# Four half buffers of edge features and four groups of accumulators in a graph kernel on one Trainium2 core

## The reference, cut to what matters

```
msg  = leaky_relu([x[dst], edge_attr] @ w1 + b1) @ w2 + b2    # layer 0
agg0 = segment_sum(msg, src)
coef = rel_table[edge_type]                                    # layer 1: weight of an edge
out1 = segment_sum(coef * alpha * z[src], dst)
out2 = segment_sum(h[src] * norm, dst)                         # layer 2
out3 = segment_sum(h[src], dst) / degree                       # layer 3
```

## Time and profile before

| | us |
|---|---|
| median of three runs | 4012.09 (4009.74 to 4016.07) |
| profiled execution, its own time | 4007.71 |
| its span, first to last instruction | 4006.0 |
| first and last indirect DMA of the scatter | 278.0 and 1541.3 |
| first and last sum of the edge tiles on DVE | 1560.5 and 3032.7 |

### The profile page before, as it was taken

How to read it: one execution, slowest core, us unless ns; L and a number is a source line. 1 busy time by engine, 2 the same in 40 slices (tenths; PEclk the granted TensorE clock), 3 DMA queues, 4 the chain that set the end, 5 groups by cost and what they waited for, 6 DMA issues and landing times. The chain is left out here.

```text
span 4006.0 us, 89562 instructions
## 1 busy us (share of the span) xinstructions
PE 2767.3 (69%) x19674; PEld 2009.0 (50%) x19675; DVE 2620.8 (65%) x7923; ACT 1608.0 (40%) x4084; POOL 1983.2 (50%) x2354
## 2 busy tenths in 40 slices
PE   2314554455454555888888888888888967769599
PEld 2213333333333334787777877787785222234345
DVE  8724555555555554888888888888886759950501
ACT  1001222222222223776777777776775613320201
POOL 0015666566666666777777777777772000000100
PEclk9955556666666657999999999999999979979797
DMA  9971222221222223777777777777774848848082
GB/s 387 415 291 59 65 65 63 64 62 61 64 64 65 65 64 106 205 203 202 204 204 203 202 206 202 202 205 197 202 206 171 294 173 295 296 151 325 22 325 100
DMA packets 702415, 696.60 MB, mean 174 GB/s; under 512 B 51182, under 2 KB 633536, under 8 KB 692640
## 3 DMA queue, kind: packets, MB, share of 16 engines
q1 hardware_dynamic: 672706, 637.13, 50.5%
q0 software_dynamic: 25792, 54.52, 4.0%
q10 hardware_dynamic: 3870, 4.37, 0.3%
HBM read 340.91 MB, written 354.90 MB: 174 GB/s over the span
## 5 line engine op out<-in xcount | busy, mean ns | idle before, releaser
L885 POOL DMA_INDIRECT sorted_rows<-rows,posi x806 | 779.8, 967 | 577.1 <-issue 246.4
L836 PE MATMUL s_peq<-sb_w1bb,eT 128*128 128x256 f32 x806 | 395.5, 591 | 584.9 <-ACT eT L703 359.6
L1166 DVE SCALAR_TENSOR_TENSOR acc<-acc,keep,pm 128x256 f32<-128x256 f32 x1504 | 717.4, 477 | 76.3 <-DVE acc L1166 36.3
L997 POOL TENSOR_SCALAR ohs_e<-iota,rt 128x128 f32<-128x128 f32 x1128 | 669.6, 608 | 11.4 <-DMA rt<-sorted_rows 11.4
L1093 PE MATMUL pm<-ohw_e,ohs_e 128*128 128x128 f32 x3008 | 662.7, 302 | 0.0
L1006 POOL TENSOR_TENSOR hid<-pre_e,excess 128x512 f32<-128x512 f32 x376 | 498.7, 1326 | 313.5 <-ACT excess L1033 313.5
L836 PEld LDWEIGHTS s_peq<-sb_w1bb,eT 128*128 128x128 f32 x806 | 188.9, 288 | 635.3 <-ACT eT L703 398.7
L1099 PE MATMUL px<-PN,dT 128*128 x4512 | 498.5, 219 | 0.2 <-ACT dT L1040 0.2
L1049 ACT ACTIVATE ohw_e<-ohd_e,rt 128x128 f32<-128x128 bf16 x1504 | 474.6, 386 | 0.0
L1092 PE MATMUL pm<-ohd_e,ohs_e 128*128 128x128 bf16 x1504 | 334.3, 222 | 198.1 <-DVE acc L1166 182.8
L1093 PEld LDWEIGHTS pm<-ohw_e,ohs_e 128*128 128x128 f32 x3008 | 459.7, 193 | 0.0
(11 more groups left out here) (299 smaller groups left out, 4469.3 us busy)
## 6 DMA issues: line engine op xcount, KB each, us to landing
count_matrices<-acc SPq DMA_DIRECT2D x1504, 128.0 KB, 2.0
ab<-count_matrices SPq DMA_DIRECT2D x75, 1600.0 KB, 7.8
sorted_rows<-zrow SPq DMA_DIRECT2D x188, 528.0 KB, 9.9
rt<-sorted_rows SPq DMA_DIRECT2D x376, 264.0 KB, 3.0
arb<-count_matrices SPq DMA_DIRECT2D x25, 1664.0 KB, 6.8
arb<-count_matrices SPq DMA_DIRECT2D x25, 1536.0 KB, 6.4
ef<-in_edge_attr_dram SPq DMA_DIRECT2D x60, 364.0 KB
sorted_rows<-rows,posi POOLq DMA_INDIRECT x806
```

The source lines that it names most:

```text
L836: nc.tensor.matmul(pe_q[:, q % 2, 0:2 * D], eT[:, q % 2, :], w1bb[:], start=True, stop=True).then_inc(s_q, 1)
L885: pool.indirect_dma_start(sortd, bass.IndirectOffsetOnAxis(ap=posi[:, h, c:c + 1], axis=0), rows[:, h, c, :], None).then_inc(s_sc[h], 16)
L997: last = nc.gpsimd.tensor_scalar(ohs[:, k, j, :], iota128[:], rt[:, k, j, D + 1:D + 2], None, ALU.is_equal)
L1166: nc.vector.scalar_tensor_tensor(acc[:, k % 2, j, :], before, keep[:, at:at + 1] if isinstance(at, int) else keep[:, ds(at, 1)], pm[:, j / ...
```

## The change: deeper rings in two parts, and another order on DVE

Scatter: `ef` gets four halves (two bodies of two). SP may load a half for body i when PE has turned the same half of body i-2; ACT loads the first two bodies, not one, at the start. The loops of SP and PE now run over two bodies a pass.

Edge tiles: `rt` gets eight groups, and the loops run over eight groups a pass on all engines. The one-hot buffers stay at four (BUFS). `acc` gets four groups (SUMS), with one semaphore a group in place of one a tile: `collect` 0 waits until all four writes of group n-4 have landed, the other three wait for none. Dummy places go from 8 to 16. On DVE collect 2 moves ahead of the destination one-hots, and collect 3 ahead of the sums.

```diff
-RING = 4
+RING = 8
+BUFS = 4
+SUMS = 4
...
-                ef = sb2("ef", [P, 2, CH, ED])
+                ef = sb2("ef", [P, 2, 2, CH, ED])
...
-                    with sp.Fori(1, whole) as i:
+                    even = whole // 2 * 2
+                    with sp.Fori(1, even // 2) as m:
+                        for b in range(2):
+                            for h in range(2):
+                                sp.wait_ge(s_te, (m * 2 + b - 2) * PAIRS + (MEET + 1, PAIRS)[h])
+                                load(sp, m * 2 + b, b, h)
+                                load_last(sp, m * 2 + b, b, h, CH)
...
-                    for h in range(2):
-                        load(act, 0, h)
-                        load_last(act, 0, h, CH)
+                    for b in range(2):
+                        for h in range(2):
+                            load(act, b, b, h)
+                            load_last(act, b, b, h, CH)
...
-                    with pe.Fori(1, BODIES - 1) as i:
-                        step(i, False, False)
+                    with pe.Fori(1, BODIES // 2) as m:
+                        for b in range(2):
+                            step(m * 2 + b, m, b, False, False)
...
-            ohd = sb("ohd_e", [P, RING, G, P], BF16)
+            ohd = sb("ohd_e", [P, BUFS, G, P], BF16)
...
-            acc = sb("acc", [P, 2, G, 2 * P])
+            acc = sb("acc", [P, SUMS, G, 2 * P])
...
-            s_w = [[sem("e_written%d_%d" % (p, j)) for j in range(G)] for p in range(2)]
+            s_w = [sem("e_written%d" % p) for p in range(SUMS)]
...
-                                     acc[:, k % 2, j, :].rearrange("p (a c) -> p a c", a=2)).then_inc(s_w[k % 2][j], 16)
+                                     acc[:, k % SUMS, j, :].rearrange("p (a c) -> p a c", a=2)).then_inc(s_w[k % SUMS], 16)
...
-                    if not (first and k < 2):
-                        dve.wait_ge(s_w[k % 2][j], (i * 2 + k // 2) * 16)
+                    if j == 0 and not (first and k < SUMS):
+                        dve.wait_ge(s_w[k % SUMS], (i * (RING // SUMS) + k // SUMS) * (16 * G))
...
                     if three:
                         st = place(*back(i, k, 3))
+                    if two:
+                        collect(*back(i, k, 2), first, 2)
                     if not (final and k >= RING - 2):
                         onehots(*back(i, k, -2), first and k + 2 < RING)
                     if two:
-                        collect(*back(i, k, 2), first, 2)
+                        collect(*back(i, k, 2), first, 3)
                     if three:
                         sums(*back(i, k, 3), first, st)
-                    if two:
-                        collect(*back(i, k, 2), first, 3)
```

More of the change, by code:

```diff
@@ L602, in build @@
                 lk = pb2("s_looked", [P, BANK])
-                s_row = [sem("s_row_a"), sem("s_row_b")]
+                s_row = [[sem("s_row%d_%d" % (b, h)) for h in range(2)] for b in range(2)]
                 s_tl = sem("s_tables_in")
@@ L625, in build @@
                 block = ctx.enter_context(nc.Block())
-                efv = ef[:].rearrange("p h c d -> p (h c d)")
+                efv = [ef[:, b, :, :, :].rearrange("p h c d -> p (h c d)") for b in range(2)]
                 rowv = rows[:].rearrange("p h c w -> p (h c) w")
@@ L956, in step @@
                     n = i * RING + k
-                    rows = loads(nc, mybir.EngineType.SP, tilei[0:1, 2, ds(n * G, G)], DUMMY + 2 * G - 1)
+                    rows = loads(nc, mybir.EngineType.SP, tilei[0:1, 2, ds(n * G, G)], DUMMY + SUMS * G - 1)
                     for j in range(G):
@@ L982, in _ @@
                     step(LOOPS - 1, k, False)
-                for p in range(2):
-                    for j in range(G):
-                        sp.wait_ge(s_w[p][j], 16 * LOOPS * RING // 2)
+                for p in range(SUMS):
+                    sp.wait_ge(s_w[p], 16 * G * (LOOPS * RING // SUMS))
             @block.gpsimd
@@ L1042, in step @@
                         negative(*back(i, k, 1), first)
-                    if not first:
-                        act.wait_ge(s_m, 2 * (n - RING) + 2)
+                    if not (first and k < BUFS):
+                        act.wait_ge(s_m, 2 * (n - BUFS) + 2)
                     act.wait_ge(s_os, n + 1)
                     act.wait_ge(s_o3, n + 1)
-                    nc.scalar.activation(ohs16[:, k, :, :], ohs[:, k, :, :], ACT.Copy).then_inc(s_o16, 1)
+                    nc.scalar.activation(ohs16[:, k % BUFS, :, :], ohs[:, k % BUFS, :, :], ACT.Copy).then_inc(s_o16, 1)
                     for j in range(G):
-                        last = nc.scalar.activation(ohw[:, k, j, :], ohd[:, k, j, :], ACT.Copy, scale=rt[:, k, j, D + 2:D + 3])
+                        last = nc.scalar.activation(ohw[:, k % BUFS, j, :], ohd[:, k % BUFS, j, :], ACT.Copy, scale=rt[:, k, j, D + 2:D + 3])
                     last.then_inc(s_ow, 1)
```

76 lines of the change are left out of this document (37 added, 39 removed).

## The result

The changed kernel takes 3949.61 us (median of four runs, 3944.23 to 3951.51); the kernel before took 4010.91 beside it (4009.32 to 4016.07). The ratio is 0.9843, with a 95% interval of 0.9825 to 0.9861. The forecast was 3969, with a range of 3938 to 4006. The profiled execution took 3951.51 us with a span of 3949.8, against 4007.71 and 4006.0 before: 56.2 us less, where the sum said 43.

What follows compares the result with a forecast made beforehand. The prediction took SP's issuing queue to bound the edge tiles and POOL to pace the scatter. Terms -54 + 7 + 1.8 + 2.0 = -43 us took 4012 to 3969 us, range 3938 to 4006.

Steps and rivals of the forecast that it cites:

- SP's queue bounds the edge tiles: Edge tiles: SP's issuing needs at least 3.83 us a group of 3.92; DVE's wait for `rt` is an effect.
- The floor, -54: Edge tiles: branch once in eight groups, so SP needs 3.78 us a group against 3.924; 54 us less.
- left-over waits, +7: Edge tiles: SP still waits 0.02 us a group, adding 7 us.
- DVE could go at 3.67: Edge tiles: without its `rt` wait and some sum waits, DVE could take about 3.67 us a group, under SP's 3.78.
- Scatter 0: Scatter: deeper `ef` removes no existing wait, so 0; length stays 1263 us between first and last indirect DMA.
- The moved collect 2, costed at nothing: Edge tiles, DVE: one-hots come 0.48 us later but hidden, so 0; without cover up to 180 us.
- Start +3.8: Start: +2.0 us for later clearing beside the second body's loads, +1.8 us for the doubled memset of `acc`.
- Layers 0: Layers after the edge tiles: code untouched, so no change, 0 us.
- B: Edge tiles: only the branch is gained, SP's small waits stay; 3994 us; chance 0.15.
- C: Loops: longer bodies no longer stay loaded and are fetched each pass; slower, 4093 to 4160 us; chance 0.08.
- D: Scatter: late loads stand behind POOL's waits for ACT, a tenth (23 us) comes back; 3946 us; chance 0.08.
- E: Edge tiles: collect 0's wait for four writes bites each group, gain falls to nothing; 4005 to 4020 us; chance 0.09.

Runs made afterwards that it cites:

- before_pad12: Kernel before with twelve semaphore increments that nobody waits for added to SP's list ahead of the edge tiles' loop; ratio 0.9911.
- edge_only: Kernel before with the edge tiles' part of the change alone, including DVE's new order, and two halves of `ef`; ratio 0.9902.
- order_only: Kernel before with only DVE's order changed (collects 2 and 3 moved); ratio 0.9998.
- ef_only: Kernel before with the scatter's part alone: four halves of `ef`, SP's and PE's scatter loops over two bodies; ratio 0.9938.
- after_sums2: Changed kernel with two groups of sums in place of four; ratio 0.9895 against the kernel before.
- unroll_only: Kernel before with SP's and PE's scatter loops over two bodies a pass, `ef` still two halves; ratio 0.9914.
- before_again: Kernel before, unedited, timed against itself and profiled on chip 3; ratio 0.9992.
- after_again: Changed kernel, unedited, run again on chip 3 against the kernel before; ratio 0.9845.
- after_ring4: Changed kernel with four groups in `rt` and in the edge tiles' loops, four groups of sums and new order kept; ratio 0.9921 against before.

## Why the prediction was right, and where it was not

**SP's queue bounds the edge tiles: right, and shown.** In the kernel after SP never waits while DVE does, and with one DMA in five taken out of SP's list the kernel before gains 2.5%, though DVE has as much to do as ever. The prediction came to this by setting SP's own list of waits beside DVE's wait for `rt`. The busy shares could not say it.

**The floor, -54, and left-over waits, +7: the size was nearly right, the split was not.** Together they made -47 and -52.3 was measured, 3.785 against 3.80 us a group. The left-over wait had been put at 0.02 us a group; it was nothing in the list. The floor of 3.78 was met. But the whole 0.47 us between 4.20 and 3.73 had been booked to the branch. In the kernel before the slow place lies in the same round as the branch, so one number held two things. About 0.2 us of it moved away with the loop: before_pad12 has no longer pass, no deeper ring, and its shortest round with the branch is 3.99 us, not 4.19. In the kernel after the branch round has a median of 4.08, not 4.20, and the slow place costs 0.18 in another round: two errors that cancel. The term came out right because the longer pass halves both costs per group, as long as it holds the slow place once in eight groups; that it holds it there is luck. The list of rounds in the prediction also leaves out one of 3.94 us (2121.80 to 2125.74 in the earlier trace rows), in which SP stood between the load and the next write.

**DVE could go at 3.67: too slow.** DVE waited 94.6 us for the writes in 1250 us, 330 groups, or 0.29 us a group; 3.785 - 0.29 is 3.50. With SP relieved it reached 3.57.

**Scatter 0: the step that failed in the first measurement.** "The prediction is wrong if [...] the scatter's length moves by more than 10 us": it moved by 18.9. The step that failed was "no wait of that stretch names a load of `ef`", and therefore 0. On chips 2 and 3 the 0 holds, 1022 us with two halves and 1021 to 1024 with four. On chips with the slow spells four halves gave 18.9 (after), and against the 1264 to 1266 of edge_only and order_only, 11 to 13 (ef_only) and 8 to 10 (after_sums2), one profiled execution each. In the first measurement 10 of the 18.9 us are POOL's waits for ACT (238.0 us before, 227.8 after), 16 are gaps without a releaser (246.4 before, 324.2 less 93.4 for the clearing after), and other waits and longer instructions take some back. A possible reason, not shown, is that PE, which then stands still for some us at a time, finds its features ready when it comes back; but the chip on which unroll_only was to tell depth from loop length had no spells. What makes the spells, and how four halves shorten the scatter under them, stays open.

**The moved collect 2, costed at nothing: right for DVE's order, blind to POOL.** Its one-hots were said to be hidden. With the new order and four row buffers they lengthened by 0.15 us a group beside POOL's `hid`, 56 us over 376 groups, which SP's bound hid; with eight they did not.

**Start +3.8: right.** +2.3 and +2.1 in the first measurement, 3.8 on chip 3.

**Layers 0: wrong by 10.6 us, most of it beside a lower clock.** Nothing there is edited. From the first load behind the last write to the end, the runs took 970 to 985 us in no order that the edits explain: 970.2 in the kernel before, 971.9 in before_again, 983.1 in before_pad12, 980.8 in the kernel after, 979.2 in after_again. Most of the 10.6 us are lost at once. The first 45 us, busy times and clock as in the earlier trace rows, in the kernel before and in the kernel after:

```profile
3035.80:3080.80 45.00, 38.00 (x186) 24.98 (x186) 23.07 (x86) 19.61 (x47) 9.08 (x8) 0.94 0.45 183
```

```profile
2968.90:3013.90 45.00, 41.17 (x153) 24.95 (x153) 19.46 (x73) 15.53 (x36) 9.09 (x8) 0.77 0.45 183
```

At the lower granted clock PE is busy longer for 153 matmuls than for 186 at the higher one. The same `nbias` instruction of DVE starts at 3073.37 us in the kernel before (L1457), 37.6 us into the layers, and at 3014.24 us in the kernel after (L1464), 45.3 us into them: 7.7 us later. All 14 profiles go the same way: 37.6 us at a clock of 0.94 (the kernel before, twice), 40.0 to 41.7 at 0.84 to 0.90, 44.2 to 44.7 at 0.80, and 45.3 at 0.77, order_only included, whose edge tiles are hardly faster. PE's clock was 0.99 to 1.00 in the 100 us ahead of it in each of them. In the kernel before the clock fell from 2.4 to 1.2 GHz 39 us into the layers, in the kernel after already at their first instruction. Why it falls sooner in one kernel than in another stays open, and so do the differences behind this stretch.

**The rivals.** B (only the branch, 3994) fell: SP's list has no wait in any profile with eight row buffers and the loads on SP (after, after_again, edge_only, after_sums2), and 25.4 us with four (after_ring4). C (refetched bodies) fell: 55 instruction packets, and rounds of 3.73 us. The Trainium skill (Runtime: NRT & Kernel Launch, Instruction fetch mechanics) had it so; the trace agrees for bodies of twice the length. D (the scatter gains) held in part on one kind of chip. E (collect 0 waits for four writes) came as a line in the list, 94.6 us, and not as a cost.

So 19 us of the gain in the first measurement came from where none was forecast, 5 more from the edge tiles, and the layers took 11 back: -43 became -56 in the span. The median fell 5 us more than the span, since the runs of after lie below its profiled one and those of before above theirs.

## What to carry to other kernels

An engine that issues DMAs has no busy share, so read its own list of waits and the distance between its issues before you believe another engine's wait: here DVE's 66 us for `rt`, and later its 95 us for the writes, were both the shadow of a full SP queue. When such a queue is the bound, deeper rings only remove its last waits and branches; moving one DMA in five to an engine with room gained 2.5% alone and 2.4% on top of the rings. And judge an edit of 1% by its stretches and on more than one chip, since moving a loop by twelve instructions gave 0.9%.

## What the runs showed of the hardware that was not expected

- SP's loop of the edge tiles ran some 0.2 us a pass slower when it held one of two places in its list that lie 128 instructions apart (near 77 and 205; 15.29 to 15.31 us for the shortest rounds against 15.08 to 15.11). Twelve idle instructions ahead of the loop made the kernel 0.9911 of its time.
- In two of the four measurements, while POOL issued indirect DMAs one after another, DVE and SP started an instruction only every 0.7 us in spells of 8 to 16 us, and in the spell shown ACT started nothing for 8.8 us and PE no matmul for 5.4. The scatter takes 1263 to 1266 us there and 1022 in the others, with the same code. That is most of why the kernel before takes 4011 and 3998 us in these two, and 3787 and 3784 in the two others.
- VectorE's one-hots (bf16, 128 x 512) took 1.60 us on average when they started inside GpSimd's `hid` (58 of 320 in order_only), and 0.69 otherwise. The Trainium skill (GPSIMD Engine Reference, Specifications) says that the two engines share their access to SBUF when VectorE reads two inputs there, as the one-hots do; these rows agree, but no run varied it.
- A DMA costs SP 0.37 to 0.39 us to issue, and five of them with the instructions around them make 3.73 us: an issuing queue can be fuller than any computing engine.
- With no edit there, the first stretch of the layers took 37.6 us at a granted clock of 0.94 and 45.3 us at 0.77.
